# A gated SSM and mixture-of-experts kernel: other orders in the prologue, and the softplus in halves

## The reference, cut to what matters

```
def _ssm_forward(hidden, z, ...):                      # hidden: ctx (512 x 256), z: layernorm(x)
    x  = in_proj_w @ hidden                            # 512 channels
    u  = silu(causal_conv(x, 4 taps) + conv_b)
    x_dbl = x_proj_w @ u                               # 16 dt rows, 16 B rows, 16 C rows
    delta = softplus(dt_proj_w @ dt_lo + dt_proj_b)
    A = -exp(A_log)                                    # 512 x 16
    for t in range(512):                               # a scan over the tokens
        state = state * exp(delta_t * A) + (delta_t * u_t) * B_t
        y_t   = sum_n state * C_t
    return (y + D * u) * silu(z)
x1  = x + tanh(g_xattn) * ssm
out = x1 + tanh(g_ffn) * moe(layernorm(x1))
```

## Time and profile before

| what | us |
|---|---|
| median of 3 runs (lowest, highest) | 1738.85 (1738.04, 1742.68) |
| the profiled execution: its own time | 1740.07 |
| its span, first to last instruction | 1738.3 |
| PE busy | 1581.6 (91%) |
| DVE busy | 1171.5 (67%) |
| POOL busy | 719.9 (41%) |
| ACT busy | 621.4 (36%) |
| mean granted TensorE clock | 0.965 of full |

### The profile page before, as it was taken

One profiled execution on the slowest core, in us unless ns is written; L12 is line 12 of the kernel. 1 busy time (PEld: TensorE's weight loads), 2 busy tenths in 40 slices (PEclk: granted clock), 3 DMA queues, 4 the chain that ended last, 5 costly groups with the idle time before them and its releaser, 6 DMA issues.

```text
span 1738.3 us, 19493 instructions
## 1 busy us (share of the span) xinstructions
PE 1581.6 (91%) x6856; PEld 1162.7 (67%) x6856; DVE 1171.5 (67%) x1629; ACT 621.4 (36%) x973; POOL 719.9 (41%) x524
## 2 busy tenths in 40 slices
PE   4676778888888899999999999999999999999999
PEld 2243456566666667777777777677767787777776
DVE  5786847588898885578888857588888653333333
ACT  5543334444454433433343334443343311111111
POOL 2465513169888850137677601167777100000000
PEclk7798979989999999999999999999999999999999
DMA  3344625878878766558665554756666357456652
GB/s 132 126 165 169 251 81 184 268 264 286 281 260 284 270 239 237 195 201 276 242 223 199 195 189 167 240 211 233 235 238 234 129 199 239 168 192 219 212 189 82
DMA packets 109888, 365.15 MB, mean 210 GB/s; under 512 B 20000, under 2 KB 45600, under 8 KB 94048
## 3 DMA queue, kind: packets, MB, share of 16 engines
q1 hardware_dynamic: 100320, 330.09, 54.3%
q10 hardware_dynamic: 9472, 33.82, 5.7%
HBM read 293.62 MB, written 70.25 MB: 209 GB/s over the span
## 4 chain that ended last, share of the span: by engine, by line
PE 63%; DVE 19%; ACT 7%; issue 6%; DMA 2%; POOL 2%; SPq 0%; ACTq 0%; DVEq 0%; POOLq 0%
PE b_g L653 14%; PE b_u L653 13%; PE b_u L744 7%; DVE ring L1389 4%; PE b_q L744 4%; PE b_q L699 3%; PE b_g L744 3%; DVE ring L1395 3%; PE b_g L717 3%; PE b_g L684 2%; DVE tt L1363 2%; PE b_g L677 2%; ACT b_a L878 1%; PE b_d L636 1%; DVE z L1363 1%
## 5 line engine op out<-in xcount | busy, mean ns | idle before, releaser
L1286 POOL TENSOR_TENSOR ring<-du,rep 128x512 f32<-128x512 f32 x256 | 335.4, 1315 | 199.1 <-DVE du L1464 115.5
L653 PE MATMUL b_g<-xnb,gm 128*128 128x512 f32 (+1 forms) x1440 | 358.2, 398 | 3.0 <-DVE tt L1363 1.5
L653 PE MATMUL b_u<-xnb,gm 128*128 128x512 f32 (+1 forms) x1440 | 349.4, 391 | 1.4 <-DVE xx L1363 1.4
L1389 DVE TENSOR_TENSOR_SCAN ring<-b_a,ring 128x512 f32<-128x512 f32 x256 | 310.6, 1213 | 55.4 <-ACT b_a L878 42.9
L1295 POOL TENSOR_TENSOR yx<-yx,ring 128x512 f32<-128x512 f32 x192 | 262.3, 1366 | 147.7 <-DVE ring L1395 146.5
L653 PEld LDWEIGHTS b_g<-xnb,gm 128*128 128x128 f32 (+1 forms) x1440 | 253.6, 180 | 92.0 <-issue 27.0
L653 PEld LDWEIGHTS b_u<-xnb,gm 128*128 128x128 f32 (+1 forms) x1440 | 257.0, 179 | 73.1 <-DVE xx L1363 2.2
L1363 DVE SCALAR_TENSOR_TENSOR tt<-tt,b_g 128x512 f32<-128x512 f32 (+1 forms) x120 | 81.9, 683 | 208.7 <-ACT tt L878 208.5
L878 ACT ACTIVATE b_a<-delta,a_neg 128x512 f32<-128x512 f32 x256 | 171.8, 679 | 79.1 <-DVE ring L1389 77.0
L744 PE MATMUL b_u<-dwt,hhl 128*128 128x512 f32 (+1 forms) x720 | 186.4, 395 | 0.4 <-DVE hhl L1366 0.4
L878 ACT ACTIVATE tt<-b_g 128x512 f32<-128x512 f32 (+1 forms) x120 | 71.2, 593 | 288.6 <-PE b_u L684 261.0
(11 more groups left out here) (214 smaller groups left out, 2153.2 us busy)
## 6 DMA issues: line engine op xcount, KB each, us to landing
gm<-scr_gm SPq DMA_DIRECT2D x60, 1024.0 KB, 7.8
dwt<-scr_dw SPq DMA_DIRECT2D x30, 1536.0 KB, 6.8
rep<-bc_d ACTq DMA_DIRECT2D x64, 512.0 KB, 5.0
gm<-scr_gm SPq DMA_DIRECT2D x30, 768.0 KB, 4.4
dqt<-scr_dq SPq DMA_DIRECT2D x24, 896.0 KB, 9.6
scr_gm<-gm SPq DMA_DIRECT2D x20, 1024.0 KB, 7.4
scr_dw<-dwt SPq DMA_DIRECT2D x10, 1536.0 KB, 6.2
qat<-scr_qa SPq DMA_DIRECT2D x24, 512.0 KB, 10.6
```

What stands on the lines that cost most here:

```text
L653: i = mm(out_b[0:IW[m], :], w, v, start=(n == 0), stop=(n == 11 and not is_routed(s)))
L1286: v.tensor_tensor(ring[:, T % NRING], du[:, T % 4, :], rep[:, N % NREP, 0], ALU.mult).then_inc(pool_dbu, 1)
L1389: v.tensor_tensor_scan(w, ba[T % 2][:], w, 0.0, ALU.mult, ALU.add).then_inc(dve_scan, 1)
```

## The change

The prologue's statistics go to the front of DVE's order (behind the load of x, ahead of the low part that `in_proj` needs), and the square root to the front of ACT's; the low parts of u are shared by POOL and DVE; relu moves from ACT to DVE for batch 0; the softplus of batch 0 runs half by half (`softplus_0`), and the first two tiles wait for the first half only. `exps` issues `exp_tile(T + 1)` ahead of `c_copy`, in all batches. The mask products are cut in five pieces, one expert's take 9 tiles, and expert 0's stand ahead of the scan; mask and adapter loads are separate (`stage_mu`, `stage_qa`), and the raw loads and `gq_store` stand elsewhere in SP's order. The end of the prologue works by channel block, through four banks, with two of the four `norm_x1` on DVE; the first body's matmuls wait for one channel block each. In the main part `exp_abs` is in halves, and in the bodies around the next batch's softplus ACT and DVE take some pieces in another order.

```diff
 # PE
-            def mask_products(e, j):   # j = 0, 1: 8 matmuls each (4 pairs), j = 1 with 8 more for the adapters
+            def mask_products(e, k):
+                if k == 0:
+                    pe.wait_ge(act_mu, e + 1)
+                if k == 4:
+                    pe.wait_ge(dma_mq, 16 * (e + 1))
...
+                j = k // 2
+                pe.wait_ge(dma_stg[j], 16 * (e + 1))
+                for c in (2 * (k % 2), 2 * (k % 2) + 1):
...
-            pe.wait_ge(act_d_u, HC)
-            for dc in range(HC):
-                mm(four[dc][:], ident, y[:, dc, :], start=True, stop=False, skip_group_check=True)
+            mask_T(0)
+            for k in range(5):
+                mask_products(0, k)
             for T in range(64):
-                if T % 8 == 0:
-                    mask_T(T // 8)
-                if T % 8 in (2, 5):
-                    mask_products(T // 8, T % 8 // 5)
+                e, p = T // 9 + 1, T % 9
+                if e < NF and p == 0:
+                    mask_T(e)
+                if e < NF and 2 <= p < 7:
+                    mask_products(e, p - 2)
+                if T < HC:
+                    pe.wait_ge(act_d_u, T + 1)
+                    mm(four[T][:], ident, y[:, T, :], start=True, stop=False, skip_group_check=True)
+            def xn_transposed_0():
+                for k, tc in enumerate((0, 2, 1, 3)):
+                    pe.wait_ge(dve_nx if tc >= 2 else act_nx, tc % 2 + 1)
...
             def up(s, m, j):
...
+                    if m == 0 and j == 0 and s % NX == 0:
+                        pe.wait_ge(dve_xnl, HC * (s // NX) + c + 1)
 # ACT
             def exps(nb, Ts):
                 for T in Ts:
+                    if T < 63:
+                        exp_tile(nb, T + 1)
                     if T % 4 == 0:
                         c_copy(nb, T // 4)
-                    if T < 63:
-                        exp_tile(nb, T + 1)
...
             def exp_abs(nb):
-                act.wait_ge(act_abs, HC * (nb + 1))
-                f(du, du, ACT.Exp, scale=-1.0).then_inc(act_ev, 1)
+                for q in range(2):
+                    act.wait_ge(act_abs, HC * nb + 2 * (q + 1))
+                    f(du[:, half[q], :], du[:, half[q], :], ACT.Exp, scale=-1.0).then_inc(act_ev, 1)
...   # shared_1, after dt_evac (routed body 0: hi("qa") now ahead of log_w, hi("dq") behind it)
-                    for n in range(NREP):
-                        rep_load(b + 1, n)
-                    exp_abs(b + 1)
-                aw_hi(s + 1)
-                if b == 0:
-                    hi("gm2", 2)
-                    hi("qb", 2)
+                aw_hi(s + 1)
+                if b == 0:
+                    hi("qb", 2)
+                if pre_:
+                    exp_abs(b + 1)
+                if b == 0:
+                    hi("gm2", 2)
+                if pre_:
+                    for n in range(NREP):
+                        rep_load(b + 1, n)
...   # prologue
             rounded(ss, aw[:]).then_inc(act_z0, 1)
+            root(0)
+            f(tgf[:], cs[:, C_GF:C_GF + 1], ACT.Tanh).then_inc(set_act, 1)
             in_evac(0, range(HC))
             conv_tanh(0, range(HC))
             u_hi(0, range(HC))
-            root(0)
...
             log_w(0)
-            d_u(0)
+            mu_copy(0)
+            d_u(0, (0, 1))
             exp_tile(0, 0)
             for T in range(64):
                 exps(0, (T,))
+                if T == 0:
+                    d_u(0, (2, 3))
...
+                if T % 9 == 2 and T // 9 + 1 < NF:
+                    mu_copy(T // 9 + 1)
+                if T == 1:
+                    gq_round(0)
+                if T % 9 == 0 and T > 0:
+                    gq_round(T // 9)
 # DVE, prologue
+            dve.wait_ge(dma_x, 16)
+            for c in range(LC):
+                row_sums(0, xx[0], c)
+            variances(0)
             dve.wait_ge(act_pre, 1)
             lo(pr[:, 1, 0:PRE_XP], pre_raw[:, 0:PRE_XP], pr[:, 0, 0:PRE_XP]).then_inc(dve_lo_in, 1)
...
+            scales(0, True)
             conv(0, 0)
             conv(0, 1)
             make_u(0, range(HC))
+            u_lo_0((1, 3))
...
             lo_state(0)
+            relu_0()
             one_plus(0)
-            rest_of_w(0)
-            softplus(0)
-            delta_u(0)
+            softplus_0(0)
+            softplus_0(1)
             for T in range(64):
                 steps(0, (T,))
-                if T % 8 == 1 and T > 8:
-                    gq_split(T // 8 - 1)
+                if T == 1:
+                    gq_split(0)
+                if T % 9 == 0 and T > 0:
+                    gq_split(T // 9)
...
+            norm_x1_0((2, 3))
...   # routed body 0: aw_low and lo_piece("qb") moved here from the end of shared_1;
...   # lo_piece("qa", s + 1) now directly behind lo_piece("dw", s), ahead of rest_of_w, softplus, delta_u
 # SP
             for e in range(1, NF):
+                stage_mu(e)
                 stage(e, 0)
                 stage(e, 1)
-                stage_mask(e)
-                gq_store(e - 1)
+                stage_qa(e)
                 if e == 1:
                     raw_load_0(0)
                     raw_load_0(1)
-                elif e < 4:
-                    raw_load_0(e)
+                elif e == 3:
+                    raw_load_0(2)
+                elif e == 5:
+                    raw_load_0(3)
+                gq_store(e - 1)
```

More of the change, by code:

```diff
@@ L224, in gated_ssm_moe @@
                              "act_relu"))
+        dve_ul, dve_relu, dve_nx = (sem(n) for n in ("dve_ul", "dve_relu", "dve_nx"))
         act_ev, dve_w, act_ln, dve_du, act_d_u = (sem(n) for n in ("act_ev", "dve_w", "act_ln", "dve_du", "act_d_u"))
@@ L865, in _ @@
             y_transposed(0)
-            xn_transposed(0, range(HC))
+            xn_transposed_0()
             for b in range(B):
@@ L980, in log_w, with d_u @@
                     f(y[:, half[q], :], w_e[q], ACT.Ln).then_inc(act_ln, 1)
-            def d_u(nb):
-                for m in range(HC):
-                    act.wait_ge(dve_w, 8 * nb + 4 + m // 2 + 1)
+            def d_u(nb, ms):
+                for m in ms:
+                    act.wait_ge(dve_w, 8 * nb + 5 + m // 2 if nb > 0 else 4 + 3 * (m // 2))
                     f(y[:, m, :], u_of(nb)[:, m, :], ACT.Copy, scale=cs[:, C_D + m:C_D + m + 1]).then_inc(act_d_u, 1)
@@ L1038, in soft_rows, with mu_copy @@
                 f(wT, b_q[0:NE, :], ACT.Copy).then_inc(act_wT, 1)
+            def mu_copy(e):
+                act.wait_ge(pe_mu, e + 1)
+                need(act, pe_gq, e)
+                f(muT[:, :, HALF:P].rearrange("p c (k r) -> p c k r", r=NR)[:, :, :, 0:3],
+                  b_d[:].rearrange("p (c a r) -> p c a r", c=HC, r=NR)[:, :, 0:NK, 0:3], ACT.Copy).then_inc(act_mu, 1)
             def gq_round(e):
@@ L1141, in routed @@
                 h_hi(s, 0)
+                if split_next:
+                    hi("qa", s + 1)
+                if more and e == 0:
+                    log_w(nb)
                 if split_here:
                     hi("dq", s)
-                if more and e == 0:
-                    log_w(nb)
-                if split_next:
-                    hi("qa", s + 1)
                 slot("b")
@@ L1161, in routed @@
                 if more and e == 0:
-                    d_u(nb)
+                    d_u(nb, range(HC))
                     exp_tile(nb, 0)
@@ L1229, in _ @@
                     tanh_z(0, (T - 8) // 4)
-            gq_round(NF - 1)
             root(1)
-            norm_x1(0, range(LC))
+            norm_x1(0, (0, 1))
             xn_hi(0, range(HC))
@@ L1269, in ctx_lo, with u_lo @@
                     lo(ctx_l[c], ctx_raw[:, c], ctx_h[c]).then_inc(pool_ctx, 1)
-            def u_lo(nb):
-                for m in range(HC):
+            def u_lo(nb, ms):
+                for m in ms:
                     pool.wait_ge(act_u, HC * nb + m + 1)
@@ L1321, in _ @@
                         lo_piece("gm%d" % m, 1)
-                u_lo(nb)
+                u_lo(nb, range(HC))
                 if b == 0:
@@ L1638, in routed @@
                     lo_piece("dw", s)
+                if split_here and e == 0:
+                    lo_piece("qa", s + 1)
                 if more and e == 0:
@@ L1650, in routed @@
                     lo_piece("dq", s)
-                if split_next:
+                if split_next and e > 0:
                     lo_piece("qa", s + 1)
@@ L1721, in _ @@
             c_mult(0, 63)
-            gq_split(NF - 1)
             gated(0)
             add_ssm(0)
+            variances(1)
             scales(1, False)
+            norm_x1_0((2, 3))
             xn_lo(0, range(HC))
```

147 lines of the change are left out of this document (91 added, 56 removed).

## The result

| | before | after |
|---|---|---|
| median of 4 runs (lowest to highest), us | 1738.44 (1737.86 to 1742.68) | 1700.81 (1696.97 to 1702.32) |
| the profiled execution: own time, span | 1740.07, 1738.3 | 1701.69, 1699.9 |
| mean granted TensorE clock | 0.965 | 0.971 |

The ratio is 0.9775, with a 95% interval of 0.9752 to 0.9798: 2.25% faster. The forecast was 1707, the range 1688 to 1728.

A forecast was written before the change was run, and what follows sets the result against it. VectorE, idle behind ScalarE and GpSimd, was taken to bound batch 0's scan, TensorE the part after 700 us. Start +3, scan -21, prologue's end -7, main part -8.2 sum to -33.2 from 1740.07: forecast 1707, range 1688 to 1728.

The forecast's parts named there:

- The low part's delay: Start: in_proj's low part, behind statistics that wait for x, begins at 14.9 in place of 10.21 us, +4.7.
- The two steps costed at nothing: Start: the softplus in halves, and u's low parts split between VectorE and GpSimd; each forecast at net 0.
- the 27.1 us: Batch 0's scan: VectorE's idle time waiting for ScalarE's exponential, all of it claimed to go.
- the lumps of idle time put back: Scan: mask pieces 5 us, GpSimd's pieces 3.5, ScalarE's work 5, first tiles 2.5, half clock 2.
- rival (a): Scan: TensorE takes VectorE's place through low clock or pieces that don't fit; 16 us gained, 1724; chance 0.17.
- The SP stall: Scan: SP stood in a raw load before issuing a mask load; 8.2 us of VectorE's waiting, claimed to go.
- The order: Main part: exponential ahead of `c_copy` takes 9.7 us off VectorE, 6.5 reaching TensorE, plus 3 behind 700 us.
- The other edits: Main part: reordered pieces around the softplus, 1.7 us of a wait staying and about 3 us later; net +1.3.
- TensorE's 10.2 us for `qat`: Main part, batch 0's routed body 0: TensorE's wait for piece `qa`, which now comes ahead of the softplus; 1.7 stay.
- (b): Main part: the `qa` wait goes wholly and VectorE's waits reach TensorE in full; 10 to 15 more, 1694; chance 0.17.
- (c): Scan: B and C rows land too late and hold GpSimd and the scan; gain gone, up to 1745; chance 0.04.
- (d): Scan: ScalarE's new order brings nothing, as `c_mult` then waits for `c_copy`; 1728; chance 0.04.

## Why the prediction was right, point by point

| step | predicted, us | measured, us |
|---|---|---|
| start, to the first scan | +3 (0 to 5) | +4.8 |
| scan | -21 (137; 122 to 155) | -25.1 (132.7) |
| end of the prologue | -7 (4 to 9) | -7.6 (20.2) |
| main part | -8.2 (0 to 18) | -10.5 |
| sum, profiled execution | 1706.9 | 1701.7 |

The number is closer than its parts: too small a loss at the start stands against too small gains in the other three.

**The start.** The low part's delay was sized right (4.7 against 4.9). That is the loss: undoing the order brought the first scan 5.2 to 5.8 us earlier. From x_proj to the first exponential the gain is 1.8, as predicted (28.61 to 43.53 before, 34.52 to 47.61 after). The two steps costed at nothing ate it. Low part to x_proj took 1.0 longer, but most of that is spread: with the code of before it took 18.40, 19.19 and 19.19 us. Exponential to first scan took 0.7 longer, and that is the change: it is 15.40 to 15.43 in the three kernels with the old softplus and 16.13 to 16.15 in all with the new one, but for the one with GpSimd's product held back (15.75). So the halves, as they are coded, were not worth nothing: they cost 0.7 us. By the mean of the kernels with either start the whole loss is 4.0 us.

**The scan.** That the 27.1 us would go was right to 3.1; the lumps of idle time put back were too large. Predicted: 18 us over VectorE's work and the one `gq_split` (119). Measured: 13.8, of which 7.0 lie behind GpSimd, where the pieces, GpSimd's own and the first tiles had 11, and 3.1 + 1.6 (`gq_split` waiting for `gq_round`) behind ScalarE, where 5 were expected; the other 2 are not traced. The mean granted clock was 0.96 and not lower than before (0.91), so rival (a) failed. The prediction's reason for that, the waits before `mask_T`, isn't enough. TensorE's waits before `mask_T` did go, from 25.8 us to 6.7. But with `c_copy` first in batch 0 they are 7.3, as good as gone, and the clock is 0.91 all the same, while with the pieces in lumps it is 0.96. What brings the clock down there stays open. The SP stall was sized too small: 8.2 was read from ScalarE's row alone, while mending it gave 10.1, as GpSimd's products waited for the same thing.

**The end of the prologue.** Last product to the statistics: 9.05 before, 5.46 after, 3.6 gained (predicted 3 to 3.5). norm_x1 to the matmuls: 9.06 to 5.41 (predicted 3.7 to 4.2, measured 3.65), plus 0.3 in the matmuls. The experiment undid the second part and lost 4.8. The early gating was not tried by itself.

**The main part.** The order was put at 9.7 us on VectorE and 9.5 at the end; taken out it cost 13.8, put into the kernel before it gave 11.3. The stretches tell which term was off: behind 700 us the order was put at 3 and gives 7.2, while before it 6.5 stands against 3.8 to 6.4. The other edits were put at +1.3, which these runs can't tell from nothing. TensorE's 10.2 us for `qat` went, and 6.9 us of the next wait came at line 781 (`issue` in the profile: the matmuls need the hidden part that VectorE ends at 328.45, and start at 328.55), which was foretold. The chain `qb`, `gm2`, `dw` is there too (ScalarE waits 9.6 us for `dw`), but behind it stands `qa`'s landing, so mending the chain alone gave nothing that can be told.

**The rivals.** (a) fails on the stage's length and on the clock. (b) would have shown `qat`'s wait gone with none behind it; the 6.9 us speak against it, though the order did reach the end more fully than forecast, which is half of what it said. (c): GpSimd waits for no B row in the scan after, at a DMA share of 0.65. (d): no product with C in the scan waits for anything.

## What to carry to other kernels

When an engine in strict order must issue a thing that the next step of a recurrence waits for and a thing that is needed one step later, put the first one first: one swapped pair, alone, gave some 21 us of the change's 38. Read the idle time of the bounding engine by what ended it, then look in the timeline for what stood in front of the releaser; an engine two steps off (here SP, held by a buffer wait ahead of an unrelated load) can be the cause of waits charged to others, and of more of them than the first row shows. A moved block costs what its own wait delays: statistics that wait for x belong behind what doesn't.

## What the runs showed of the hardware

A VectorE instruction with both operands in SBUF and a GpSimd one excluded each other whole, and the price fell on whichever came second: VectorE's half-steps took 2.18 and 2.19 us in place of 1.23 while GpSimd's two products ran, and these two took 4.41 us where two of them take 2.5. The record of the first begins at 57.09, behind a VectorE instruction begun at 56.93. The Trainium skill ("SBUF — State Buffer", SBUF: two separate sides) states this lock; the trace agrees, and by the durations the lock passed to and fro, one instruction each, although each VectorE step follows the one before within 0.03 us. Keeping the engines apart saved 1.9 us of VectorE's time but only 0.39 us of the way to the first scan: the scan then waited for the product.
